# Layer-0 preparation of an adaLN and mixture-of-experts kernel in two halves

## The chip, the cores and the metric

The kernel runs on one core of a Trainium2 chip. The metric is the device time of one execution in microseconds. TensorE (PE), VectorE (DVE), ScalarE (ACT) and GpSimd (POOL) each run one instruction stream in order; SyncE (SP) issues most DMAs, also in order. The streams meet only at semaphores.

## The reference, cut to what matters

Two layers are computed, each a per-sequence product of x with a gathered matrix and then a feed-forward network of experts, with residual sums. The change touches layer 0 alone. With N = 2048 tokens, D = 512, hidden width 2048, E = 8 experts of rank 8, for both choices k of the router:

```python
def _L0_ffn_ref(hidden_states, W_r, b_r, W1, b1, W2, b2, A1, B1, A2, B2):
    probs = jax.nn.softmax(x @ W_r.T + b_r, axis=-1)
    w_topk, idx_topk = jax.lax.top_k(probs, K)
    base1 = x @ W1.T + b1
    u1 = jnp.einsum('nd,erd->ner', x, A1)
    for k in range(K):
        oh = jax.nn.one_hot(idx_topk[:, k], E, dtype=x.dtype)
        z1 = (u1 * oh[:, :, None]).reshape(N, E * R)
        h = act(base1 + z1 @ B1_rf * SCALING)
        u2 = jnp.einsum('nf,erf->ner', h, A2)
        z2 = (u2 * oh[:, :, None]).reshape(N, E * R)
        y = h @ W2.T + b2 + z2 @ B2_rf * SCALING
        res = res + w_topk[:, k:k + 1] * y
```

Layer 1 is a per-sequence product with a bias, and a routed expert network beside a shared one. It is the same before and after.

## The kernel before

The 2048 tokens are four super-tiles (s, or n in the preparation) of 512, each of TPS = 4 tiles of 128; J = 16 is the number of tiles. The 2048 hidden units are FT = 16 chunks f of 128, so layer 0 has 64 hidden tiles i = 16 s + f. Every fp32 operand is kept as a high and a low half, and a product is three matmuls: high by high, high by low, low by high.

**Preparation.** For each super-tile `cond_x(n)` gives the transposed product in ps_y (TensorE); ScalarE's `high_x` and VectorE's `low_x` split it. `router_and_u1(n)` (12 matmuls) gives the router's logits and the low-rank product u1 in ps_h; ScalarE copies the logits to lg_t, `logit_rows` (TensorE) turns them, `logits` (VectorE) brings them to SBUF. u1 is copied by VectorE (`u1_rows`) and a second time by ScalarE. `route(k, js)` on VectorE is a chain of small operations with one `Exp` on ScalarE between them: it finds both experts and both weights. The first call does the 4 tiles of super-tile 0, the second the 12 others. It ends with the masks' operands (mexp_first, mexp_rest) which `masks` on TensorE turns and ScalarE copies to m_base and m_step; `place_z` on VectorE multiplies u1 by them. `rho_rows` turns the ratio of the weights; SP stores it to DRAM and `load_weights` brings it back over all partitions as wb.

**Weights.** Of each chunk SP loads w_raw; ScalarE (`high_w2`, `high_w1`), VectorE (`low_w2`) and GpSimd (`low_w1`) split it into w2_hi, w2_lo (kept) and w_hl (two buffers), and SP stores w_hl to w1s_d, from where super-tiles 1 to 3 load it again. `high_w1(f)` for f of 2 or more waits for the store that frees its buffer.

**Hidden tiles.** `step` on TensorE is: `hidden` of tile i (12 matmuls on x, 2 on z), half of `down` of tile i - 1 (8), `second` (2), the other half of `down` (8): 32 matmuls. ScalarE does two gelus for each tile, VectorE `hidden_tile` (multiply by wb, add, and two splits). PSUM is full: ps_h has 2 banks, ps_y 4 (which `down` accumulates in over a super-tile), ps_u 2. In `super_tile(0)` all of `rho_rows(1)` and `masks(1)` to `masks(3)` stand between `second` of tile 1 and `down` of tile 0, and use ps_y.

The order on each engine is written out by hand. TensorE's before is: cond_x 0 and 1, router 0, cond_x 2, router 1, cond_x 3, router 2, rho_rows 0, masks 0, router 3, logit_rows 2, hidden_x 0, logit_rows 3, hidden_x 1, hidden_z, super-tiles.

Of the kernel before, what the change touches and what calls it, by code (L numbers as in the profile page):

```python
# [23 lines left out]
def adaln_ffn(nc, x, itok0, itok1, side, cond0, router0, router0_b, w1b, b1, b2, b2s,  # L24
# [34 lines left out]
    with ExitStack() as top:  # L59
# [47 lines left out]
        rho_t = [sb(f"rho_t{k}", [n, P]) for k, n in enumerate((TPS, J - TPS))]  # L107
# [30 lines left out]
        zz = sb("zz", [P, SUP])  # L138
        zq = sb("zq", [P, SUP])
# [95 lines left out]
        bd_in_act = sem("bd_in_act")  # L235
# [5 lines left out]
        u1_twice = sem("u1_twice")  # L241
# [150 lines left out]

        def lgt_at(n, j=0):

            return (n * TPS + j) * 2 * E
# [32 lines left out]
        def _(sp):  # L428
# [8 lines left out]
            def load_bd(n):  # L437
                for j in range(TPS):
                    load_block(sp, n, j, 0, bd_in[n][0])
# [26 lines left out]
            load_bd(1)  # L466
            load_w1(0)
            for n in range(2, NS):
                sp.wait_ge(cond_done, 1 + (n - 1) * DC)
                load_x(n)  # L470
                load_bd(n)
            load_w1(1)
            for n in range(2, NS):
                sp.wait_ge(xt_lo_done, 4 + (n + 1) * DC)
                for half, dst in zip(xt_of(n), (xt_hi_d, xt_lo_d)):
                    sp.dma_start(dst[n - 2], half.rearrange("p c n -> p (c n)").bitcast(F32)).then_inc(xt_st[n % 2], 16)
                if n == 2:
                    sp.wait_ge(wt_sb, 1)
                    sp.dma_start(wrow_d[0:TPS, :], rho_t[0][:]).then_inc(wrow_st, 16)
                    sp.wait_ge(wrow_st, 16)  # L480
                    load_weights(0)
# [25 lines left out]

            for s in range(NS):
                for f in range(FT):
                    nxt = s * FT + f + 2  # L510
                    if nxt < FT:
                        load_w1(nxt)
                    if s == 0:
                        store_w1(f)
                    if FT <= nxt <= STEPS:
                        load_w1s(nxt)
                    if s == 0 and f == 2:
                        sp.wait_ge(wt_sb, 2)
                        sp.dma_start(wrow_d[TPS:J, :], rho_t[1][:]).then_inc(wrow_st, 16)
                        sp.wait_ge(wrow_st, 32)  # L520
                        load_weights(1)
                    if s and f == 1:
                        store_x1(s - 1)
                    if s == 0 and f == XRES_AT:

                        sp.wait_ge(g_done, 3)
# [71 lines left out]
        def _(pool):  # L598
# [160 lines left out]
        def _(act):  # L759
# [5 lines left out]
            for j in range(TPS // 2, TPS):  # L765
                load_block(act, 0, j, 1, bd_in_act)
# [34 lines left out]
            def exps(k, js):  # L801
# [3 lines left out]
            def masks(n):  # L805
                s, k = n // 2, n % 2
                act.wait_ge(mt_done, n + 1)
                nc.scalar.copy((m_base, m_step)[k][:, s * SUP:(s + 1) * SUP], ps_y[:, n % 4, :]).then_inc(mt_read, 1)

            def rho_rows(k):  # L810
                act.wait_ge(w01t_done, k + 1)
                nc.scalar.copy(rho_t[k][:], ps_u[0:(TPS, J - TPS)[k], 1, (k + 2) * P:(k + 3) * P]).then_inc(wt_sb, 1)
# [20 lines left out]
            def gelus(i, f, u, sums=None):  # L833
                b = bias1[:, f:f + 1]
                act.wait_ge(a_done, i + 1)
                act.wait_ge(g_done, i + 1)
                nc.scalar.activation(h0[u][:], ps_h[:, u, :], ACT.Gelu_apprx_tanh, bias=b).then_inc(h0_done, 1)  # L837
                if sums is not None:
                    move_sums(sums)
                act.wait_ge(z_done, i + 3)  # L840
                act.wait_ge(g1_done, i + 1)
                nc.scalar.activation(h1[u][:], ps_h[:, u, :], ACT.Gelu_apprx_tanh, bias=b).then_inc(h1_done, 1)  # L842

            for f in range(FT):
                gelus(f, f, f % 2)
                if f == 1:
                    rho_rows(1)
                    for n in range(2, 2 * NS):
                        masks(n)
# [3 lines left out]
            def move_sums(s):  # L853

                for j, t in enumerate((zz, zq)):
# [120 lines left out]
        def _(dve):  # L976
# [7 lines left out]
            dve.wait_ge(small_in, 16 * 5)  # L984
            nc.vector.tensor_copy(ur_hi[:, :, 0:ER + E], ur_raw[:]).then_inc(split_small, 1)
            nc.vector.tensor_copy(b2s_hi[:], b2s_raw[:]).then_inc(split_small, 1)
            dve.wait_ge(split_small, 2)
            nc.vector.tensor_tensor(ur_hi[:, :, ER + E:UR], ur_raw[:, :, ER:ER + E],
                                    ur_hi[:, :, ER:ER + E].bitcast(F32), ALU.subtract).then_inc(split_small, 1)
            nc.vector.tensor_tensor(u1_lo[:], ur_raw[:, :, 0:ER], ur_hi[:, :, 0:ER].bitcast(F32), ALU.subtract)\  # L990
                .then_inc(split_small, 1)
            nc.vector.tensor_tensor(b2s_lo[:], b2s_raw[:], b2s_hi[:].bitcast(F32), ALU.subtract).then_inc(split_small, 1)

            def low_x(n):
                hi, lo = xt_of(n)
                for c in range(DC):
# [26 lines left out]
            def softmax(rt, rc, parts, bias, r_max, r_exp, js=slice(0, J), turn=1):  # L1023
# [6 lines left out]
                tt(l, p, over_e(m), ALU.subtract).then_inc(r_max, 1)  # L1030
                dve.wait_ge(r_exp, turn)
# [847 lines left out]
```

## Time and profile before

| what | value |
|---|---|
| median of 3 runs | 1081.24 us (1078.67 to 1088.08) |
| the profiled execution, its own time | 1079.91 us |
| its span, first to last instruction | 1078.3 us |
| mean granted TensorE clock | 0.986 |
| TensorE busy | 1025.1 us |
| VectorE busy | 545.7 us |
| ScalarE busy | 308.9 us |
| GpSimd busy | 353.6 us |

The execution's own time is 1.6 us longer than its span. Engines overlap, so busy times don't add up. A start in a row is counted from the span's first instruction.

### The profile page before, as it was taken

The numbers are of one execution on the slowest core, as the hardware profiler recorded it, in microseconds if no ns is written. First come the engines' busy times: TensorE is split into PE (matmuls) and PEld (weight loads), VectorE is DVE, ScalarE is ACT, GpSimd is POOL, SyncE is SP. The second block draws the span as 40 slices with busy tenths as digits, with TensorE's granted clock in tenths as the row PEclk, the third lists the DMA queues.
The fourth block names the chain that finished last, engine by engine and source line by source line (L and its number), as shares of the span: only waits on it lengthen the run. The fifth ranks groups of instructions, "written<-read, shape, count | busy, mean of one in ns | idle before, by whom it ended". The sixth has DMA issues, their size and how long they took to land.

```text
span 1078.3 us, 14931 instructions
## 1 busy us (share of the span) xinstructions
PE 1025.1 (95%) x4922; PEld 842.2 (78%) x4923; DVE 545.7 (51%) x888; ACT 308.9 (29%) x542; POOL 353.6 (33%) x349
## 2 busy tenths in 40 slices
PE   7879999999999999999978999999999999999993
PEld 5668888788878888788845777778878989998993
DVE  3777776555475445654475443484553344452100
ACT  2443332211121121212123110210034444454551
POOL 3113335430000000000024000003058889888873
PEclk9989999999999999999999999999999999999997
DMA  7566652543434334432336110101446665556433
GB/s 210 205 184 215 193 183 87 164 142 128 146 117 139 125 140 154 156 128 88 107 130 235 42 40 1 40 1 55 162 159 158 153 148 115 148 130 158 76 61 39
DMA packets 51371, 136.42 MB, mean 127 GB/s; under 512 B 8788, under 2 KB 10052, under 8 KB 50820
## 3 DMA queue, kind: packets, MB, share of 16 engines
q1 hardware_dynamic: 37700, 109.55, 30.1%
q0 software_dynamic: 12368, 25.68, 12.0%
q10 hardware_dynamic: 1264, 0.72, 0.4%
q8 instruction: 19, 0.31, 0.1%
q14 instruction: 20, 0.16, 0.0%
HBM read 96.85 MB, written 39.07 MB: 126 GB/s over the span
## 4 chain that ended last, share of the span: by engine, by line
PE 72%; DMA 8%; DVE 6%; POOL 6%; issue 3%; SPq 1%; ACT 1%; PEldq 0%; POOLq 0%; DVEq 0%; PEld 0%; ACTq 0%
DMA out_x<-yt,slot_tok 7%; PE ps_y L1543 6%; PE ps_y L1545 6%; PE ps_y L1544 6%; PE ps_h L1507 5%; PE ps_h L1506 5%; PE ps_h L1505 5%; PE ps_u L1551 3%; PE ps_u L1550 3%; PE ps_y L1694 2%; PE ps_y L1695 2%; PE ps_h L1678 2%; POOL xg L700 2%; PE ps_h L1679 2%; PE ps_h L1680 2%
## 5 line engine op out<-in xcount | busy, mean ns | idle before, releaser
L1103 DVE TENSOR_TENSOR h<-h,wb 128x512 f32<-128x512 f32 x64 | 45.6, 713 | 176.0 <-ACT h L842 175.9
L837 ACT ACTIVATE h<-ps_h,bias 128x512 f32<-128x512 f32 x64 | 44.1, 690 | 238.8 <-PE ps_h L1514 238.7
L1543 PE MATMUL ps_y<-w_hi,g_hi 128*128 (+1 forms) x256 | 102.3, 400 | 3.0 <-DVE g_lo L1111 3.0
L1505 PE MATMUL ps_h<-xt_hi,w_hl 128*128 128x512 f32 x256 | 100.6, 393 | 2.0 <-POOL w_hl L625 2.0
L1545 PE MATMUL ps_y<-w_hi,g_lo 128*128 (+1 forms) x256 | 101.6, 397 | 0.0
L1544 PE MATMUL ps_y<-w_lo,g_hi 128*128 (+1 forms) x256 | 101.5, 396 | 0.0
L1507 PE MATMUL ps_h<-xt_hi,w_hl 128*128 128x512 f32 x256 | 101.0, 394 | 0.0
L1506 PE MATMUL ps_h<-xt_lo,w_hl 128*128 128x512 f32 x256 | 100.9, 394 | 0.0
L1329 DVE CAST eg_hi<-e_raw 128x704 fp32r<-128x704 f32 x32 | 21.1, 717 | 123.5 <-PE ps_y L1790 112.4
L842 ACT ACTIVATE h<-ps_h,bias 128x512 f32<-128x512 f32 x64 | 44.0, 688 | 116.3 <-PE ps_h L1527 116.3
L711 POOL DMA_INDIRECT out_x<-yt,slot_tok x39 | 63.4, 1625 | 27.7 <-DMA out_x<-yt,slot_tok 18.5
L643 POOL DMA_DIRECT2D s_raw<-in_sgu x8 | 4.3, 547 | 195.1 <-DVE g_lo L1111 190.6
L717 POOL TENSOR_TENSOR xg_lo<-xg_f,xg_hi 128x512 fp32r<-128x512 f32 x39 | 59.5, 1526 | 14.9 <-ACT xg_f L924 13.4
L1543 PEld LDWEIGHTS ps_y<-w_hi,g_hi 128*128 128x128 f32 x256 | 48.3, 188 | 15.5 <-DVE g_lo L1111 2.7
L1505 PEld LDWEIGHTS ps_h<-xt_hi,w_hl 128*128 128x128 f32 x256 | 48.5, 190 | 13.3 <-ACT lg_t L797 2.1
L1116 DVE TENSOR_TENSOR g_lo<-h,g_hi 128x512 fp32r<-128x512 f32 x64 | 56.9, 888 | 2.2
L1545 PEld LDWEIGHTS ps_y<-w_hi,g_lo 128*128 128x128 f32 x256 | 48.3, 189 | 11.7
L1544 PEld LDWEIGHTS ps_y<-w_lo,g_hi 128*128 128x128 f32 x256 | 48.4, 189 | 11.4
L1506 PEld LDWEIGHTS ps_h<-xt_lo,w_hl 128*128 128x128 f32 x256 | 48.3, 189 | 11.2
L1507 PEld LDWEIGHTS ps_h<-xt_hi,w_hl 128*128 128x128 f32 x256 | 48.5, 189 | 10.5
L729 POOL TENSOR_TENSOR rgt_lo<-rgt_f,rgt_hi 128x384 fp32r<-128x384 f32 x39 | 54.8, 1406 | 5.3 <-ACT rgt_f L942 5.3
L1760 PE MATMUL ps_y<-eg_hi,xg_hi 128*128 x156 | 53.5, 345 | 0.0
(303 smaller groups left out, 2485.1 us busy)
## 6 DMA issues: line engine op xcount, KB each, us to landing
w_hl<-w1s_d SPq DMA_DIRECT2D x49, 704.0 KB, 4.1
w1s_d<-w_hl SPq DMA_DIRECT2D x16, 704.0 KB, 6.0
e_raw<-in_wgu SPq DMA_DIRECT2D x8, 1408.0 KB, 7.6
w_raw<-in_w1b SPq DMA_DIRECT2D x16, 608.0 KB, 4.7
x_in<-in_x SPq DMA_DIRECT2D x4, 1024.0 KB, 7.1
xres<-in_x SPq DMA_DIRECT2D x16, 256.0 KB, 4.4
x_d<-xres SPq DMA_DIRECT2D x4, 1024.0 KB, 7.5
acc<-x_d SPq DMA_DIRECT2D x4, 1024.0 KB, 7.8
```

Of the source, the lines that this page charges most:

```text
L711: pool.indirect_dma_start(out=out, in_=yt[t % 4][:], in_offset=None, out_offset=bass.IndirectOffsetOnAxis(ap=slot_tok[:, t:t + 1], axis=0) ...
L717: nc.gpsimd.tensor_tensor(xg_lo[:].rearrange("p c n -> p (c n)"), xg_f[:], xg_hi[:].rearrange("p c n -> p (c n)").bitcast(F32), ALU.subtract)\
L729: nc.gpsimd.tensor_tensor(rgt_lo[:].rearrange("p c n -> p (c n)"), rgt_f[:], rgt_hi[:].rearrange("p c n -> p (c n)").bitcast(F32), ALU.sub ...
L1103: tt(h1[u][:], h1[u][:], wb[:, v, :], ALU.mult).then_inc(gch, 1)
L1116: tt(g1_lo[u][:], h1[u][:], g1_hi[u][:].bitcast(F32), ALU.subtract).then_inc(g1_done, 1)
L1505: mm(ps_h[:, u, :], w_chunk(u, 0, c), xt_hi[v][:, c, :], start=(c == 0), stop=False)
L1506: mm(ps_h[:, u, :], w_chunk(u, 0, c), xt_lo[v][:, c, :], start=False, stop=False)
L1507: mm(ps_h[:, u, :], w_chunk(u, 1, c), xt_hi[v][:, c, :], start=False, stop=False)
L1543: mm(ps_y[:, j, :], g_hi[u][:, cols], sl(w2_hi), start=first, **kw)
L1544: mm(ps_y[:, j, :], g_hi[u][:, cols], sl(w2_lo), start=False, **kw)
L1545: mm(ps_y[:, j, :], g_lo[u][:, cols], sl(w2_hi), start=False, **kw)
L1760: mm(o, xg_hi[:, c, :], w(eg_hi, c), start=(c == 0), stop=False)
```

## The change

1. Routing goes by halves of 8 tiles (super-tiles 0 and 1, then 2 and 3). The first route is woven with the splits of super-tiles 2 and 3 (`meanwhile`, `split`); the second stands on VectorE behind hidden tile 1, and its `Exp` on ScalarE behind the first four gelus.
2. Masks are made by super-tile: 0 and 1 in the preparation (ps_y), 2 and 3 in super-tiles 1 and 2 (ps_u), each with its own operands (`spread_masks`).
3. On TensorE routers 0 and 1 stand together; hidden_x of tile 1 goes ahead of rho_rows and masks 0; router 3, into ps_u, has both `second` between its halves; then masks 1, logit_rows 3 and `down` of tile 0.
4. ScalarE copies u1 twice straight from PSUM, and splits w1 and w2 of chunks 0 and 1 ahead of the masks; VectorE's `low_w2` 0 and 1 also go ahead.
5. On SP both stores of split x go ahead of the store of rho and of wb; chunks 2 and 3 of the weights and the second wb follow. Some loads of bd change queue.

```diff
             def logits_and_u1(n):
                 act.wait_ge(u1_done, n + 1)
                 act.wait_ge(lgt_done, n)
-                nc.scalar.copy(lg_t[:], ps_h[ER:UR, n % 2, :]).then_inc(lgt_cp, 1)
-                act.wait_ge(u1_read, n + 1)
-                nc.scalar.copy(u1t[ER:P, n * SUP:(n + 1) * SUP], u1t[0:ER, n * SUP:(n + 1) * SUP]).then_inc(u1_twice, 1)
+                rows = u1_bank(n)
+                nc.scalar.copy(lg_t[:], rows[ER:UR]).then_inc(lgt_cp, 1)
+                nc.scalar.copy(u1t[0:ER, n * SUP:(n + 1) * SUP], rows[0:ER])
+                nc.scalar.copy(u1t[ER:P, n * SUP:(n + 1) * SUP], rows[0:ER]).then_inc(u1_read, 1)
...
             high_x(0)
             high_x(1)
             logits_and_u1(0)
+            high_w1(0)
+            logits_and_u1(1)
             high_x(2)
-            exps(0, slice(0, TPS))
-            logits_and_u1(1)
+            exps(0)
             high_x(3)
+            high_w1(1)
+            high_w2(0)
+            high_w2(1)
             logits_and_u1(2)
+            nc.scalar.activation(h0[0][:], zero16[:], ACT.Gelu_apprx_tanh).then_inc(warm, 1)
             rho_rows(0)
             masks(0)
-            masks(1)
-            for f in range(2):
-                high_w2(f)
-                high_w1(f)
-            logits_and_u1(3)
-            exps(1, slice(TPS, J))
-            nc.scalar.activation(h0[0][:], zero16[:], ACT.Gelu_apprx_tanh).then_inc(warm, 1)
             act.wait_ge(warm, 1)
...
+            for f in range(2):
+                gelu_first(f, f, f)
+            for f in range(2):
+                gelu_second(f, f, f)
+            high_w1(2)
+            logits_and_u1(3)
+            masks(1)
+            high_w2(2)
+            high_w2(3)
+            high_w1(3)
+            exps(1)
+            for f in range(2, FT):
                 gelus(f, f, f % 2)
...
+                    if s == 1 and f == 1:
+                        rho_rows(1)
                     gelus(s * FT + f, f, f % 2, s - 1 if f == 1 else None)
+                    if s + 1 < NS and f == 1:
+                        masks(s + 1)
...
             low_x(0)
+            split_constants()
             low_x(1)
-            u1_rows(0)
-            low_x(2)
             logits(0)
-            route(0, slice(0, TPS))
-            u1_rows(1)
+            low_x(2, range(0, 2))
             logits(1)
-            low_x(3)
-            u1_rows(2)
+            route(0, split=True)
+            spread_masks(0, [m[:, 0:TPS] for m in mexp_first])
+            low_w2(0)
+            low_w2(1)
             logits(2)
             place_z(0)
             place_z(1)
-            u1_rows(3)
-            low_w2(0)
-            low_w2(1)
-            logits(3)
-            route(1, slice(TPS, J))
+            spread_masks(1, [m[:, TPS:2 * TPS] for m in mexp_first])
...
                         hidden_tile(f, v, f % 2)
+                        if f == 0:
+                            logits(3)
...
+                        if f == 1:
+                            route(1)
...
+            sp.wait_ge(wt_sb, 1)
+            sp.dma_start(wrow_d[0:J // 2, :], rho_t[0][:]).then_inc(wrow_st, 16)
+            sp.wait_ge(wrow_st, 16)
+            load_weights(0)
+            for f in range(2):
+                load_w1(f + 2)
+                store_w1(f)
+            load_weights(1)
...
             cond_x(0)
             cond_x(1)
             router_and_u1(0)
-            cond_x(2, between=0)
             router_and_u1(1)
-            cond_x(3, between=1)
+            logit_rows(0)
+            cond_x(2, between=1)
+            cond_x(3)
             router_and_u1(2)
+            pe.wait_ge(lgt_cp, 2)
+            pe.wait_ge(u1_read, 2)
+            hidden_x(1, 0, 1, None)
+            pe.wait_ge(xt_lo_done, 4 + NS * DC)
             rho_rows(0)
-            pe.wait_ge(xt_lo_done, 4 + NS * DC)
             masks(0)
-            router_and_u1(3)
             logit_rows(2)
-            for u in range(2):
-                pe.wait_ge(lgt_cp, 3 + u)
-                pe.wait_ge(u1_read, 3 + u)
-                if u:
-                    logit_rows(3)
-                hidden_x(u, 0, u, None)
+            pe.wait_ge(u1_read, 3)
+            hidden_x(0, 0, 0, None)
             hidden_z(0, 0)
+            hidden_z(0, 1)
+
+            def seconds():
+                second(0, 0, 0)
+                second(1, 0, 1)
+
+            router_and_u1(3, between=seconds)
             for s in range(NS):
                 super_tile(s, s % 2)
```

In `super_tile(s)` for s of 1 or more TensorE now does `second` of the first tile, `sums_end(s - 1)`, for s = 1 `rho_rows(1)`, `second` of the second tile, `masks(s + 1)`, and then `down`.

## Rows read from the trace of the kernel before

**Rows 1.** Page, part 1: busy time, share and instructions.

```profile
PE 1025.1 (95%) x4922; PEld 842.2 (78%) x4923; DVE 545.7 (51%) x888; ACT 308.9 (29%) x542; POOL 353.6 (33%) x349
```

**Rows 2.** Windows of 30 us: stretch, each engine's busy us, then clock, DMA share, GB/s.

```profile
30.00:60.00 30.00, 22.83 (x118) 16.35 (x116) 22.70 (x65) 13.22 (x24) 4.23 (x4) 0.94 0.62 226
60.00:90.00 30.00, 26.06 (x118) 20.87 (x119) 21.05 (x35) 12.33 (x22) 8.74 (x8) 0.89 0.57 174
90.00:120.00 30.00, 30.00 (x132) 24.37 (x131) 24.24 (x32) 10.67 (x16) 10.24 (x9) 1.00 0.68 211
```

**Rows 3.** Timeline of TensorE: start, duration, instruction, idle before and releaser.

```profile
39.24 0.27 PE L1480 MATMUL ps_u<-ident,rho 128*4 128x128 f32 x1
41.85 0.62 PE L1490 MATMUL ps_y<-ident,mexp_first 128*128 128x128 bf16 x8 [2.33 <-DVE w_lo L998]
...
47.61 0.55 PE L1505 MATMUL ps_h<-xt_hi,w_hl 128*128 128x512 f32 x1 [2.00 <-POOL w_hl L625]
...
58.71 0.50 PE L1526 MATMUL ps_h<-z_step,w_hl 128*128 128x512 f32 x1 [1.41 <-ACT h L837]
...
61.99 0.80 PE L1526 MATMUL ps_h<-z_step,w_hl 128*128 128x512 f32 x1 [2.55 <-ACT h L837]
...
63.34 2.25 PE L1490 MATMUL ps_y<-ident,mexp_rest 128*128 128x128 bf16 x24
67.53 0.47 PE L1543 MATMUL ps_y<-w_hi,g_hi 128*128 128x512 f32 x1 [1.95 <-DVE g_lo L1111]
...
72.87 0.39 PE L1505 MATMUL ps_h<-xt_hi,w_hl 128*128 128x512 f32 x1
...
80.28 0.39 PE L1505 MATMUL ps_h<-xt_hi,w_hl 128*128 128x512 f32 x1
```

**Rows 4.** Windows of 1 us (columns as in rows 2).

```profile
49.00:50.00 1.00, 1.00 (x4) 0.81 (x3) 1.00 (x1) 0.00 (x0) 0.78 (x1) 0.50 1.01 426
...
70.00:71.00 1.00, 1.00 (x4) 0.81 (x3) 0.86 (x3) 0.00 (x0) 0.00 (x0) 0.50 0.98 180
```

**Rows 5.** Timeline of VectorE.

```profile
39.31 2.48 DVE L998 TENSOR_TENSOR w_lo<-ps_y,w_lo 128x512 fp32r<-128x512 f32 x4 [1.17 <-ACT w_lo L792]
...
46.10 1.81 DVE L1071 TENSOR_TENSOR zf<-u1t,m_base 128x512 f32<-128x512 f32 x1 [0.22 <-DVE lg L1007]
...
50.36 0.69 DVE L1071 TENSOR_TENSOR zf<-u1t,m_step 128x512 f32<-128x512 f32 x1
...
54.55 0.26 DVE L1026 TENSOR_TENSOR rt_p<-lg 128x96 f32<-128x96 f32 x1
...
62.20 1.08 DVE L1061 TENSOR_SCALAR mexp_rest<-rt_l 128x1536 bf16<-128x1536 f32 x1
```

**Rows 6.** Timeline of ScalarE.

```profile
8.52 1.28 ACT L792 ACT_TABLE_LOAD   x1 [8.52 <-issue]
14.47 0.58 ACT L792 CAST xt_hi<-ps_y 128x512 fp32r<-128x512 f32 x1 [4.68 <-PE ps_y L1456]
...
56.01 1.28 ACT L830 ACT_TABLE_LOAD   x1
...
60.57 0.78 ACT L787 CAST w_hl<-w_raw 128x704 fp32r<-128x704 f32 x1
```

**Rows 7.** Waits of SP's queue, 0 to 140 us: total us, times, longest.

```profile
SPq L448 <- DMA wrow_d<-rho_t: 5.7, 2, 4.8
```

**Rows 8.** DMA issues, 43 to 62 us: times, size, median us to landing.

```profile
w1s_d<-w_hl SPq DMA_DIRECT2D x2, 704.0 KB, 7.0
...
xt_lo_d<-w_lo SPq DMA_DIRECT2D x1, 1024.0 KB, 7.7
```

**Rows 9.** Timeline where super-tile 1 begins.

```profile
187.75 0.68 ACT L837 ACTIVATE h<-ps_h,bias 128x512 f32<-128x512 f32 x1
...
189.77 0.40 PE L1526 MATMUL ps_h<-z_step,w_hl 128*128 128x512 f32 x1
...
190.75 0.19 PEld L1543 LDWEIGHTS ps_y<-w_hi,g_hi 128*128 128x128 f32 x1 [0.80 <-DVE g_lo L1111]
```

More of the change, by code:

```diff
@@ L138, in adaln_ffn @@
         zz = sb("zz", [P, SUP])
+        spread = ExitStack()
+        sb_spread = tensors(spread)
+        mexp_next = [sb_spread(f"mexp_next{k}", [P, TPS, P], BF16) for k in range(2)]
+        spread.close()
         zq = sb("zq", [P, SUP])
@@ L437, in load_bd @@
             def load_bd(n):
-                for j in range(TPS):
+                for j in range(TPS // 2 if n == 2 else TPS):
                     load_block(sp, n, j, 0, bd_in[n][0])
@@ L466, in _ @@
             load_bd(1)
+            load_bd(2)
+            sp.wait_ge(cond_done, 1 + DC)
+            load_x(2)
             load_w1(0)
[L468 to L471, printed above, removed]
+            load_bd(3)
+            sp.wait_ge(cond_done, 1 + 2 * DC)
+            load_x(3)
             load_w1(1)
@@ L845, in _ @@
                 gelus(f, f, f % 2)
[L846 to L849, printed above, removed]
                 if f + 2 < FT:
@@ L1477, in rho_rows @@
                 pe.wait_ge(w01_ok, k + 1)
-                pe.wait_ge(wt_sb, k)
-                first, many = ((0, TPS), (TPS, J - TPS))[k]
-                nc.tensor.transpose(ps_u[0:many, 1, (k + 2) * P:(k + 3) * P], rho[:, first:first + many], ident[:])\
-                    .then_inc(w01t_done, 1)
+                nc.tensor.transpose(rho_bank(k), rho[:, half_of(k)], ident[:]).then_inc(w01t_done, 1)
             def masks(s):
-                pe.wait_ge(mexp_ok, 2 if s == 0 else 4)
-                for n in (2 * s, 2 * s + 1):
-                    if n >= 4:
-                        pe.wait_ge(mt_read, n - 3)
-                    spread = mexp_rest[n % 2][:, (s - 1) * TPS:s * TPS] if s else mexp_first[n % 2][:]
+                if s == 1:
+                    pe.wait_ge(wt_sb, 1)
+                if s == 2:
+                    pe.wait_ge(wt_sb, 2)
+                for k in range(2):
+                    pe.wait_ge(mexp_ok, 2 * s + k + 1)
+                    expanded = mexp_first[k][:, s * TPS:(s + 1) * TPS] if s < 2 else mexp_next[k][:]
                     for j in range(TPS):
-                        last = mm(ps_y[:, n % 4, j * P:(j + 1) * P], spread[:, j], ident16[:], start=True, stop=True)
+                        last = mm(mask_bank(s, k)[:, j * P:(j + 1) * P], expanded[:, j], ident16[:],
+                                  start=True, stop=True)
                     last.then_inc(mt_done, 1)
@@ L1549, in down @@
                 hi, lo = ((g_hi, g_lo), (g1_hi, g1_lo))[half]
+                if first and s == 0:
+                    pe.wait_ge(lu_done, NS)
+                    pe.wait_ge(u1_read, NS)
+                if first and s in (1, 2):
+                    pe.wait_ge(mt_read, 2 * s + 3 + half)
                 mm(ps_u[:, half, :], a2, hi[u][:], start=first, **kw)
@@ L1576, in super_tile @@
                     hidden_x(base + 1, v, 1, rows)
-                hidden_z(s, 1)
-                second(base, s, 0)
-                if s:
+                    hidden_z(s, 1)
+                    second(base, s, 0)
                     sums_end(s - 1)
-                second(base + 1, s, 1)
-                if s == 0:
-                    rho_rows(1)
-                    for k in range(1, NS):
-                        masks(k)
-                    pe.wait_ge(wt_sb, 2)
-                    pe.wait_ge(mt_read, 2 * NS)
+                    if s == 1:
+                        rho_rows(1)
+                    second(base + 1, s, 1)
+                if s + 1 < NS:
+                    masks(s + 1)
+                if s == 0:
+                    logit_rows(NS - 1)
                 down(base, 0, 0, 0, s)
```

160 lines of the change are left out of this document (92 added, 68 removed).

## The prediction

> **What bounds the kernel now.** I read the page's busy times first: TensorE is busy for 1025.1 of 1078.3 us [rows 1], so only about 53 us could be won without taking matmuls away, and this change takes none away that count. Then the windows of 30 us, to see where those 53 us lie that the change can reach. From 90 us TensorE is busy in all of its 30 us at full clock; from 30 to 90 it is idle for 11.1 us (7.17 and 3.94) and its clock is 0.94 and 0.89 [rows 2]. So the change acts on a stretch that ends at about 80 us. The timeline of TensorE shows what is waited for there: 2.33 us for the split of super-tile 3, 2.00 for GpSimd's split of w1, 1.41 and 2.55 for ScalarE's first gelus, 1.95 for VectorE's first g_lo [rows 3], 10.2 us together. Behind such gaps the granted clock falls to 0.50, the 1.2 GHz level [rows 4]; in the two stretches in which it does, matmuls of 512 columns start 0.43 us apart and not 0.23. At 0.50 TensorE has lost half of what it does: some 1.7 us for each stretch of 3.4 us.
>
> I use two marks. The mark **step 2** is the start of hidden tile 2 at 72.87 us, the mark **step 3** that of tile 3 at 80.28 [rows 3]. The step between them has 32 matmuls in 7.41 us, 0.23 each, and later steps are the same. What is won at step 3 is won in the end, save what is handed to the later super-tiles.
>
> **The new order, worked through.** *Up to router 2.* TensorE's work is the same, and before it ended with the transpose of rho at 39.24 [rows 3]. Router 1 now fills the 0.5 us in which cond_x 2 waited for its DMA. I take 38.8 us: no gain worth naming. ScalarE's extra copies (u1 from PSUM) and its early `high_w1(0)` fit in gaps.
>
> *Hidden_x of tile 1.* It needs both w1 splits. ScalarE's second is behind `high_x(3)`, 36.6 to 37.4, GpSimd's then takes 1.9 to 2.5 us: 39.9. Twelve matmuls of 0.23: 42.7. The gap is 1.1 us instead of 2.33 plus 2.00.
>
> *Routing, first half.* VectorE's chain for 8 tiles, with the four splits of super-tile 3 (2.48 us, [rows 5]) inside it, is the next thing late. It has 22 small operations up to the ratio of the weights. Before, 54.55 to 62.20 were 24 of them and one spread of some 0.9 us for 12 tiles, so 0.28 us each [rows 5]; with 8 tiles I take 0.255. From 32.2 us the sum is 22 × 0.255 + 4 × 0.62 (super-tile 3) + 2 × 0.62 (the rest of super-tile 2) = 9.3 us, to 41.5, and GpSimd's split of w1 runs at that time: one operation took 1.81 us with GpSimd busy where the same takes 0.69 [rows 5], so one hit, 1.1 us (bounds: none, or two): rho and the last split at about 42.6. The masks' operands follow at 43.6, `low_w2` of 0 and 1 at 44.9. TensorE turns rho and mask 0 to 44.4, then logit_rows 2, hidden_x 0 (2.8 us, to 47.6), four z products (0.9), half of router 3 (1.4), both `second` (0.9), the other half (1.4), mask 1 (0.6): 52.8 us. `place_z` twice is 3.8 us from 45.3 (GpSimd idle), in time. What stood as two waits for gelu, 1.41 and 2.55, is now behind router 3: gone.
>
> *What is late next: the store that frees w_hl.* ScalarE has `high_w1(2)` ahead of the copy of router 3's logits. It waits for the store of chunk 0, and that stands on SP behind both stores of x, the store of rho, and wb. I follow this queue. x of super-tile 3 is split at 42.6, so its two stores of 1 MB are issued at about 42.8; rho is in SBUF at 43.4 and its store goes right behind them. Before, the two waits for a rho store were 0.9 and, behind other transfers, 4.8 us (5.7 in all, [rows 7]); with 2 MB ahead I take 4.0: 47.5. Then wb, the load of chunk 2, and the store of chunk 0 at 48.5. Such a store took 7.0 us at the median [rows 8]; the first of these was issued at 54.13, and ScalarE took the buffer without a wait at 60.57 [rows 6], so at most 6.4. I take 6.7: 55.2. Queued behind that wait on ScalarE are the logits and u1 of super-tile 3, mask 1 and the splits of w2 2 and 3; who waits for them is TensorE, for logit_rows 3, from 52.8. So: `high_w1(2)` to 56.0, logits copied 56.6, rows turned 57.1, a new gap of over 4 us. `down` of tile 0 is 16 × 0.23 = 3.7: step 2 at 60.9, against 72.87. Before, its masks for 12 tiles (2.25 us, [rows 3]) stood here too; 8 of 24 remain, ahead of the gap.
>
> *Routing, second half.* VectorE takes logits 3, waits for w2's split (60.0), does tile 1 (g_lo 62.8, all of it 64.0), another w2 split (64.6), then four operations of route: 65.7. ScalarE's `Exp` ends at 66.0. Gelu's table is loaded again: a load is 1.28 us [rows 6]. The load of Exp's table costs nothing, as ScalarE waits there anyway and a load runs ahead of the wait of its instruction: the first one ran at 8.52, the copy behind it waited for TensorE until 14.47 [rows 6]. Gelu of tile 2 then ends at 68.0, and `second` of tile 2, which TensorE reaches at 60.9 + 3.2 + 1.8 = 65.9 at full clock, starts at 68.2: a second gap of 2.3 us. With 2 + 8 more matmuls step 3 starts at 70.5. To that I add 1.5 for the clock: two gaps could cost 1.7 each behind them, but what is lost ahead of a wait costs nothing. Bounds 0 and 3.4. **Step 3 at 72.0**, 8.3 us earlier than before.
>
> On tables the traces show 1.28 us and the next instruction right behind. The Trainium skill (ScalarE: Activation LUTs, What ACT_TABLE_LOAD costs) counts 2.66 us for a switch, the drain with it, and advises to batch calls by table set, which this change stops doing: it would make the sum 1.4 us worse. In this trace the gap behind the load at 56.01 is too small for that drain, so the row decides.
>
> *Handed to later super-tiles.* Masks 2 and 3 are 16 small matmuls, 16 × 2.25 / 24 = 1.5 us, on TensorE where it has little to wait. At super-tile 1 gelu of tile 17 ran at 187.75, during `sums_end`, and `second` went at 189.77 [rows 9]; now ScalarE first waits for rho_rows(1), behind `sums_end`, copies it and only then starts that gelu: `second` is 1.4 us late. Of this and the mask, up to 0.80 at each of two places falls in the wait for g_lo that stood there [rows 9]. VectorE's two spreads (0.8 us) fall in its own idle time. Sum 1.5 + 1.4 - 1.0 = **1.9 us** (bounds 1.0 and 3.3).
>
> **Sum.** 8.3 - 1.9 = 6.4 us. Against the profiled execution's own time of 1079.91 (1.6 us over its span) that is **1073.5 us**. The median shown is 1.3 above that execution; a measurement of this kernel can tell about 1%, 11 us, from nothing.
>
> **Rivals.** (a) *The rho store is quick and the clock holds.* It speaks for this that one such store took 0.9 us, against it that 2 MB stand ahead now. Then 3.1 us off the queue, 0.3 off the store and 1.5 off the clock come on top: 1073.5 - 4.9 = 1068.6. Chance 0.18.
>
> (b) *Routing's second half gives back more.* For it: the chain now stands between tiles 1 and 2, so VectorE comes to tile 2 at about 71 us, when GpSimd splits w1 of chunk 4, and an operation then takes 1.1 us more [rows 5]; two such hits and one more slow stretch (1.7) give 3.9 us: 1077.4. Against it: a step leaves VectorE about 1.5 us. Chance 0.22. A switch of the length that the Trainium skill gives on the page named above falls among these times.
>
> (c) *The end on the other side: the SP queue.* If what was moved together on SP runs at the mean of 60 to 90 us, 174 GB/s [rows 2], and not at 426 [rows 4], then 2.1 MB of x end at 42.8 + 12.1 = 54.9, and wb, chunk 2 and the store (1.6 MB, 9.2 us) at 64.1. All after it is 8.9 us later: 1082.4. It decides from 61.6 us on: if chunk 0's store lands later than that, the change loses. Against it: in 1 us windows with a full queue the DMAs move over 400 GB/s. Chance 0.10.
>
> (d) *It doesn't do what it says*: if mask 1 and router 3 find an earlier wait (a bank of ps_y or ps_u not yet free), they stand in the open, 2.8 + 0.6 us: 1076.9. It lies in (b)'s times; both banks are free by my walk some us before. Chance 0.05.
>
> **How the numbers follow.** The forecast itself, 1071 to 1077, has 0.45. The range 1068.5 to 1081 takes in (a), (b), (d) and the bounds of rho's store (0.9 to 4.8) and of the clock, and leaves out most of (c). Faster by over 1% is below 1070.4: most of (a) and a little of the forecast's early side, 0.19. Slower by over 1% needs more than (c): 0.04. Within 1%: 0.77.
>
> **What the changed profile would show.** TensorE: hidden_x of tile 1 at about 40 us with a gap of near 1; no gap between the z products and `second`; a gap of 4 us ahead of logit_rows 3, ended by ScalarE's copy; step 2 at 61, a gap ahead of `second` of tile 2 that ends with gelu, step 3 at 72. ScalarE: two more table loads, the first hidden; `high_w1(2)` idle before it for the store of w_hl. At super-tile 1 a gap of over 1 us ahead of `second`. The prediction is wrong if `high_w1(2)` doesn't wait (a), if step 3's lead has gone by tile 5 (b), or if that store lands after 61.6 (c).

## The result and the profile after

The changed kernel takes 1074.63 us (median of 10 runs, 1070.94 to 1081.08) against 1080.74 us (10 runs) of the kernel before: a ratio of 0.9947, 95% interval 0.9921 to 0.9973. The forecast was 1073.5 us. The profiled execution has a span of 1071.6 us. One execution each of e9_w2_back (5790.24 us) and e10_spread (2060.74 us) took far longer than all others, for no reason that the record shows, and neither is counted below. TensorE's busy time, from the page, answers to [rows 1]:

```profile
PE 1020.5 (95%) x4922; PEld 840.5 (78%) x4923; DVE 534.3 (50%) x888; ACT 314.1 (29%) x548; POOL 352.1 (33%) x349
```

The matmuls are the same 4922. TensorE is busy for 4.6 us less; in a second trace of the changed kernel (e11_after_again) it is 1022.3 us, 2.8 less, so part of this is scatter. The windows of 30 us answer to the first two of [rows 2]:

```profile
30.00:60.00 30.00, 21.39 (x130) 16.71 (x131) 20.70 (x53) 15.87 (x28) 3.47 (x4) 0.90 0.63 245
60.00:90.00 30.00, 28.71 (x114) 22.55 (x113) 22.86 (x48) 13.15 (x21) 7.06 (x7) 0.93 0.57 167
```

From 30 to 90 us TensorE is now idle for 9.9 us (8.61 and 1.29) instead of 11.1, and more of the work is in the first window. By the clock column TensorE's clock is at 0.50 for as long as before, 10.2 us, but differently placed: before, in three stretches (at about 48, 62 and 68 us) in which TensorE was at work for all but 0.5 us; now in one stretch from 54.3 to 64.5, in which it has nothing to do until 59. Work at the low clock fell by about 4 us, and as it runs there at half speed, that is some 2 us of time (an estimate from these windows). TensorE's timeline shows one large gap where five middling ones stood [rows 3]:

```profile
38.98 0.47 PE L1563 MATMUL ps_h<-xt_hi,w_hl 128*128 128x512 f32 x1 [0.71 <-ACT lg_t L827]
...
50.44 0.62 PE L1547 MATMUL ps_y<-ident,mexp_first 128*128 128x128 bf16 x8
58.96 0.60 PE L1484 MATMUL ps_u<-ident,lg_t 16*128 16x16 f32 x4 [7.90 <-ACT lg_t L827]
59.49 0.80 PE L1605 MATMUL ps_y<-w_hi,g_hi 128*128 128x512 f32 x1
...
65.58 0.39 PE L1563 MATMUL ps_h<-xt_hi,w_hl 128*128 128x512 f32 x1
...
71.05 0.50 PE L1584 MATMUL ps_h<-z_step,w_hl 128*128 128x512 f32 x1 [0.27 <-ACT h L865]
...
73.48 0.39 PE L1563 MATMUL ps_h<-xt_hi,w_hl 128*128 128x512 f32 x1
...
77.88 0.50 PE L1605 MATMUL ps_y<-w_hi,g_hi 128*128 x1 [1.03 <-DVE g_lo L1161]
...
82.17 0.39 PE L1563 MATMUL ps_h<-xt_hi,w_hl 128*128 128x512 f32 x1
```

A step is the start of a hidden tile on TensorE. Step 2 (65.58) comes 7.3 us earlier than before, step 3 (73.48) 6.8 us, step 4 (82.17 against 87.67) 5.5 us. TensorE's gap of 7.90 names ScalarE's copy of the logits; what ScalarE waited for is in its own timeline (compare [rows 6]):

```profile
57.52 0.78 ACT L816 CAST w_hl<-w_raw 128x704 fp32r<-128x704 f32 x1 [7.48 <-DMA w1s_d<-w_hl]
58.33 0.58 ACT L827 COPY lg_t<-ps_u 16x512 f32<-16x512 f32 x1
...
66.72 1.28 ACT L834 ACT_TABLE_LOAD   x1
68.74 0.26 ACT L834 ACTIVATE rt_q<-rt_l 128x64 f32<-128x64 f32 x1 [0.74 <-DVE rt_l L1077]
69.02 1.28 ACT L865 ACT_TABLE_LOAD   x1
70.31 0.69 ACT L865 ACTIVATE h<-ps_h,bias 128x512 f32<-128x512 f32 x1
```

`high_w1(2)` stood 7.48 us for the store that frees its buffer, with the logits queued behind it, as forecast. SP's queue shows why the store was late:

```profile
40.92 0.32 SPq L499 DMA_DIRECT2D xt_hi_d<-w_lo  x1
41.28 0.43 SPq L499 DMA_DIRECT2D xt_lo_d<-w_lo  x1
42.41 0.33 SPq L527 DMA_DIRECT2D wrow_d<-rho_t  x1
49.29 0.34 SPq L469 DMA_DIRECT2D wb<-wrow_d  x1
...
50.15 0.43 SPq L503 DMA_DIRECT2D w1s_d<-w_hl  x1
```

Between the issue of rho's 4 KB (42.41) and that of wb (49.29), which waits for them, lie 6.9 us: the 2 MB of x stand ahead. Whether they are the cause is tested in e2 below. Where super-tile 1 begins ([rows 9]), `second` of tile 17 waits for a gelu:

```profile
184.26 0.27 PE L1536 MATMUL ps_u<-ident,rho 128*8 128x128 f32 x1
185.46 0.50 PE L1584 MATMUL ps_h<-z_step,w_hl 128*128 128x512 f32 x1 [0.93 <-ACT h L865]
...
186.46 0.48 PE L1605 MATMUL ps_y<-w_hi,g_hi 128*128 128x512 f32 x1
```

**A common zero.** The first loads land up to 3 us apart from trace to trace: the first matmul of router 0 starts at 21.46 here, 21.80 before, and between 21.6 and 24.7 in the experiments. So times in the experiments are counted from that matmul. The last mark is the first matmul of the last `sums_end`, at layer 0's end. Two traces of the same kernel (changed and e11; e6 and e12) differ at these marks by up to 0.6 us, so less than that is not read as an effect. From the last mark to the end of the span it is 522.6 to 530.0 us in these traces, though layer 1 is the same in all; so the marks settle effects in layer 0 that the whole time can't. The ratio is to the kernel before in the same series, and each series had a chip of its own (e1 to e4; e5 to e8; e9 to e12).

| from router 0, us | down of tile 0 | step 4 | last sums | ratio to before, 95% |
|---|---|---|---|---|
| before | 45.7 | 65.9 | 528.7 | |
| changed | 38.0 | 60.7 | 524.7 | 0.9947 (0.9921 to 0.9973) |
| e11_after_again | 38.3 | 61.3 | 525.2 | 0.9955 (0.9936 to 0.9975) |
| e1_act_late | 36.2 | 60.2 | 524.2 | 0.9913 (0.9883 to 0.9943) |
| e2_rho_first | 33.1 | 56.4 | 520.4 | 0.9926 (0.9896 to 0.9956) |
| e3_router_back | 38.5 | 61.2 | 525.1 | 0.9953 (0.9925 to 0.9981) |
| e4_rho_turn | 38.6 | 61.6 | 524.8 | 0.9926 (0.9898 to 0.9955) |
| e5_queue_clear | 32.3 | 55.7 | 518.9 | 0.9910 (0.9880 to 0.9941) |
| e6_all | 32.3 | 52.5 | 516.5 | 0.9885 (0.9849 to 0.9922) |
| e7_no_exp | 38.3 | 61.7 | 525.7 | 0.9962 (0.9936 to 0.9987) |
| e8_all_router_back | 33.6 | 55.0 | 519.0 | 0.9904 (0.9871 to 0.9936) |
| e9_w2_back | 38.4 | 61.2 | 525.1 | 0.9975 (0.9955 to 0.9994) |
| e10_spread | 38.2 | 59.3 | 524.1 | 0.9957 (0.9940 to 0.9975) |
| e12_all_again | 32.5 | 52.7 | 516.7 | 0.9872 (0.9853 to 0.9892) |

### The profile page after: what moved, and what is told of

The parts are those of the page before. It is cut to its first block, busy times and chain, and to the rows that moved or that the text cites. A ratio compares the mean times of both kernels' runs of the same rounds, so it can differ in the third digit from the quotient of the medians.

```text
span 1071.6 us, 14937 instructions
## 1 busy us (share of the span) xinstructions
PE 1020.5 (95%) x4922; PEld 840.5 (78%) x4923; DVE 534.3 (50%) x888; ACT 314.1 (29%) x548; POOL 352.1 (33%) x349
## 4 chain that ended last, share of the span: by engine, by line
PE 80%; DMA 5%; DVE 5%; POOL 4%; issue 2%; ACT 1%; SPq 1%; PEldq 0%; POOLq 0%; DVEq 0%; PEld 0%; ACTq 0%
PE ps_y L1605 5%; PE ps_y L1607 5%; PE ps_y L1606 5%; PE ps_h L1565 5%; PE ps_h L1564 5%; PE ps_h L1563 5%; DMA out_x<-yt,slot_tok 3%; PE ps_u L1618 3%; PE ps_u L1617 3%; PE ps_y L1766 2%; PE ps_h L1837 2%; PE ps_y L1767 2%; PE ps_y L1837 2%; PE ps_y L1832 2%; PE ps_y L1833 2%
## 5 line engine op out<-in xcount | busy, mean ns | idle before, releaser
L1564 PEld LDWEIGHTS ps_h<-xt_lo,w_hl 128*128 128x128 f32 x256 | 48.1, 188 | 11.1
L1832 PE MATMUL ps_h<-eg_hi,xg_hi 128*128 x156 | 50.9, 327 | 2.7 <-ACT xg_hi L968 1.8
```

Of the source, the lines that this page charges most:

```text
L1564: mm(ps_h[:, u, :], w_chunk(u, 0, c), xt_lo[v][:, c, :], start=False, stop=False)
L1832: mm(o, xg_hi[:, c, :], w(eg_hi, c), start=(c == 0), stop=False)
```

## Experiments on the gap: ScalarE's order and SP's queue

**e1_act_late.** ScalarE's order alone:

```diff
-            high_w1(2)
             logits_and_u1(3)
             masks(1)
+            high_w1(2)
```

> On ScalarE the split of w1 of chunk 2 goes behind the logits and masks of super-tile 3's router. Theory (ScalarE waits 7.5 us for the store of w_hl and holds the logits back): logit_rows 3 then starts at about 51.5 us and not at 59.0, and the next thing late is wb (VectorE's tile 0 starts at 54.2, g_lo at 57.0), so down of tile 0 starts at 57.1 instead of 59.5; step 3 at about 71.5 instead of 73.5, time 2 us less (ratio to before 0.993). Rival (GpSimd's split of chunk 2 and routing's second half are the bound behind it, not the logits): step 2 moves, step 3 stays at 73.5, ratio 0.995.

In TensorE's timeline the gap has moved from the logits to `down` of tile 0:

```profile
51.47 0.41 PE L1484 MATMUL ps_u<-ident,lg_t 16*128 16x16 f32 x4 [0.21 <-ACT lg_t L827]
57.85 0.79 PE L1605 MATMUL ps_y<-w_hi,g_hi 128*128 128x512 f32 x1 [5.97 <-DVE g_lo L1161]
70.55 0.50 PE L1584 MATMUL ps_h<-z_step,w_hl 128*128 128x512 f32 x1 [2.15 <-ACT h L865]
```

The logits are turned at 51.47, as the theory says, and wb is next: VectorE's tile 0 started at 55.05, after 6.5 us of waiting for it. `down` is 1.9 us earlier, but ahead of `second` of tile 2 there is now a gap of 2.15 us, and step 4 is only 0.5 us earlier, within the scatter: the rival is right about the end, and for the reason it gives. Its ratio, 0.9913, is lower than its trace accounts for.

**e2_rho_first.** SP's order alone:

```diff
+            store_xt(2)
...
             sp.wait_ge(wt_sb, 1)
             sp.dma_start(wrow_d[0:J // 2, :], rho_t[0][:]).then_inc(wrow_st, 16)
             sp.wait_ge(wrow_st, 16)
             load_weights(0)
             for f in range(2):
                 load_w1(f + 2)
                 store_w1(f)
+            store_xt(3)
             load_weights(1)
```

> On SP the two stores of x of super-tile 3 go behind the store of rho, wb, and the loads and stores of w1 that follow. Theory (the rho store took 6.9 us because 2 MB stood ahead of it): the rho store lands in about 1.3 us, wb is there at 48, the store that frees w_hl lands at about 51, ScalarE's wait falls from 7.5 to about 1, down of tile 0 starts at 53 to 54, step 2 at 57.5, step 3 at 68 to 69: 4.5 to 5.5 us less than the changed kernel, ratio to before 0.990. Rival (routing's second half gives it back): step 3 at 72 or later, ratio 0.994.

SP's queue (router 0 is at 24.66 here), and TensorE's gap:

```profile
45.56 0.33 SPq L529 DMA_DIRECT2D wrow_d<-rho_t  x1
47.84 0.34 SPq L469 DMA_DIRECT2D wb<-wrow_d  x1
...
48.70 0.43 SPq L505 DMA_DIRECT2D w1s_d<-w_hl  x1
```

```profile
57.39 0.41 PE L1487 MATMUL ps_u<-ident,lg_t 16*128 16x16 f32 x4 [3.14 <-ACT lg_t L830]
```

(`store_xt(n)` is the loop's body for super-tile n.) The rho store now holds the queue for 2.3 us instead of 6.9, the gap falls from 7.90 to 3.14, and step 4 and the last sums are 4.3 us earlier from router 0: the first theory stands, a little below its 4.5 to 5.5 us. The median ratio shows only 2 to 3 of these us; where the rest goes is open. The theory's landing time for the store of w_hl was too short: issued at 48.70, it freed ScalarE at 55.96. At tile 2 gaps of 1.64 and 1.04 us are left.

**e5_queue_clear.** Both orders, the stores of w_hl 0 and 1 ahead of rho, and the edit of e4 below:

```diff
+            store_xt(2)
+            for f in range(2):
+                store_w1_early(f)
             sp.wait_ge(wt_sb, 1)
...
             load_weights(0)
             for f in range(2):
                 load_w1(f + 2)
-                store_w1(f)
+            store_xt(3)
             load_weights(1)
```

> SP stores w_hl of chunks 0 and 1 ahead of everything that follows x of super-tile 2, then rho and wb, then the loads of chunks 2 and 3, and x of super-tile 3 last; ScalarE has the split of chunk 2 behind the masks, and the turned rho behind the gelu of tile 17. Times are counted from router 0's first matmul (the changed kernel: down of tile 0 at 38.0, step 4 at 60.7, last sums at 524.7; the second experiment 33.1, 56.4, 520.4). Theory (queue and ScalarE's wait are the whole gap): down of tile 0 at 31.5, set by g_lo; step 4 at 52, since routing's second half still stands between tiles 1 and 2; last sums at 515; ratio to before 0.986. Rival (wb, spread over 128 partitions, moves slowly and is the bound wherever it stands): down of tile 0 at 33 or later, ratio 0.990.

```profile
54.40 0.42 PE L1493 MATMUL ps_u<-ident,lg_t 16*128 16x16 f32 x4 [0.21 <-ACT lg_t L836]
56.85 0.50 PE L1614 MATMUL ps_y<-w_hi,g_hi 128*128 128x512 f32 x1 [2.04 <-DVE g_lo L1170]
```

The gap is down to 0.21 and 2.04 us. `down` of tile 0 at 32.3 lies between the two forecasts, and what is left of the wait is the rival's: VectorE stood 2.58 us for wb (whether wb is slow because it is a broadcast is another matter, taken up in the last section). The theory missed its later marks: step 4 is at 55.7 and not 52, the last sums at 518.9 and not 515. `down` of tile 0 took 5.4 us instead of 3.7, with the clock at 0.50 in part, and the gaps at tile 2 are 1.72 and 1.01 us.

## Experiments on routing's second half

**e6_all.** As e5, and the route in pieces:

```diff
-                        if f == 1:
-                            route(1)
+                        route_piece(f)
...
-            exps(1)
             for f in range(2, FT):
                 gelus(f, f, f % 2)
...
+                if f == 3:
+                    exps(1)
```

The pieces are the four operations up to `Exp` (f = 2), the three that normalize (3), the first choice (4), the second (6), and the ratio with the masks' operands (7). SP loads the residual from f = 9 and not from f = 3, as it shares the memory.

> As e5_queue_clear, and routing's second half in five pieces behind tiles 2, 3, 4, 6 and 7, its Exp behind tile 3's gelus; the loads of the residual go behind it. Theory (a step of tiles leaves VectorE some 1.5 us, and the chain of 6 us in one piece does not fit): no gap ahead of second of tile 2 nor ahead of down of tile 2, step 4 at 50.0 from router 0, last sums at 513, ratio to before 0.984, 2 us less than e5_queue_clear. Rival (the pieces push g_lo over its slack in five steps): five small gaps of 0.5 us, and no gain over e5_queue_clear.

```profile
56.95 0.50 PE L1638 MATMUL ps_y<-w_hi,g_hi 128*128 128x512 f32 x1 [2.12 <-DVE g_lo L1195]
```

This is the last gap of TensorE that its timeline lists up to 100 us. Both gaps at tile 2 are gone, step 4 is 3.2 us earlier than in e5 and the last sums 2.4 us. Instead of the rival's five small gaps there is one, of 0.54 us at 103.2. Both of the theory's marks were missed, 50.0 by 2.5 us and 513 by 3.5, as e5 missed its own by 3.7 and 3.9; against e5 it gains 3.2 and 2.4 us where 2 were forecast.

**e10_spread.** The same pieces alone in the changed kernel, with the `Exp` and the loads of the residual moved as in e6.

```diff
-                        if f == 1:
-                            route(1)
+                        route_piece(f)
...
-            exps(1)
...
+                if f == 3:
+                    exps(1)
```

> The changed kernel with routing's second half in five pieces behind tiles 2, 3, 4, 6 and 7 and its Exp behind tile 3's gelus, nothing else changed. Theory: down of tile 0 stays at 38.0 from router 0, the gaps of 0.27 and 1.03 ahead of second and down of tile 2 go, step 4 at 59.2 instead of 60.7, last sums at 523.3. Rival (the tiles catch up later anyway, so the gaps only move): last sums at 524.5.

Step 4 at 59.3 is as forecast and both gaps at tile 2 are gone. At the last sums, 524.1 against 524.7 and 525.2 of the two traces of the changed kernel, 0.6 to 1.1 us are left, little more than the scatter, of 1.4 forecast: part is given back, as the rival says, and one gap of 0.54 us ahead of a later `down` has appeared.

**e7_no_exp.** Is it the table switch that costs there?

```diff
-                nc.scalar.activation(rt["q"][:, js], rt["l"][:, js], ACT.Exp).then_inc(r_exp, 1)
+                nc.scalar.activation(rt["q"][:, js], rt["l"][:, js], ACT.Copy if k else ACT.Exp).then_inc(r_exp, 1)
```

> The changed kernel with a plain copy in place of the second Exp, so that gelu's table stays: the weights of super-tiles 2 and 3 are then wrong. Theory (the first load runs while ScalarE waits, the second ends 0.3 us after TensorE gets there): the gap ahead of second of tile 2 goes, the one ahead of down of tile 2 stays as VectorE's chain sets it, step 4 at 60.3 to 60.7 from router 0, ratio as for the changed kernel. Rival (a switch costs 2.7 us with its drain): step 4 1.5 us or more earlier.

The gap ahead of `second` went, as the theory says. But step 4 was not earlier: it is 1.0 us *later* than in the first trace of the changed kernel and 0.4 later than in the second, since the gap ahead of `down` of tile 2 grew to 2.68 us. VectorE's timeline, and below it GpSimd's:

```profile
67.54 1.50 DVE L1075 TENSOR_TENSOR rt_p<-rt_p,rb_rows 128x64 f32<-128x64 f32 x1
69.08 0.22 DVE L1076 TENSOR_REDUCE rc_m<-rt_p 128x8 f32<-128x64 f32 x1
...
74.51 1.59 DVE L1117 TENSOR_TENSOR oh_step<-rt_oh,oh_base 128x64 f32<-128x64 f32 x1
```

```profile
67.39 1.57 POOL L653 TENSOR_TENSOR w_hl<-w_raw,w_hl 128x640 fp32r<-128x640 f32 x1
...
74.45 1.57 POOL L653 TENSOR_TENSOR w_hl<-w_raw,w_hl 128x640 fp32r<-128x640 f32 x1
```

Two operations that take 0.23 us elsewhere took 1.50 and 1.59, each beside a split of w1 on GpSimd. The changed kernel has two such hits as well:

```profile
67.47 1.23 DVE L1077 TENSOR_TENSOR rt_l<-rt_p,rc_m 128x64 f32<-128x64 f32 x1
...
75.80 1.93 DVE L1161 TENSOR_TENSOR g_lo<-h,g_hi 128x512 fp32r<-128x512 f32 x1
```

These two stand beside GpSimd's splits of 67.06 and 75.38 and take 1.23 us instead of 0.22 and 1.93 instead of 0.69. Without the tables TensorE was earlier (step 3 by 0.7 and 1.3 us against the two traces), and with it GpSimd's second split, which then fell on the end of the chain and not on g_lo behind it. VectorE's path to g_lo of tile 2 became no shorter, so the time won at `second` was lost again at `down`. Each of the two switches is a load of 1.28 us, and the first was hidden. Together they were worth the gap ahead of `second`, 0.27 us in the first trace and 0.92 in the second, and nothing at step 4. There is no room in ScalarE's timeline for the 2.66 us that the Trainium skill (ScalarE: Activation LUTs, What ACT_TABLE_LOAD costs) counts: a load at 69.02 ends at 70.30 and gelu starts at 70.31.

## Experiments on two of the change's moves

**e3_router_back.** The placing of router 3 around `second` undone in the changed kernel:

```diff
             logit_rows(2)
+            pe.wait_ge(lu_done, 3)
+            router_and_u1(3)
             pe.wait_ge(u1_read, 3)
             hidden_x(0, 0, 0, None)
             hidden_z(0, 0)
             hidden_z(0, 1)
-            router_and_u1(3, between=seconds)
+            second(0, 0, 0)
+            second(1, 0, 1)
```

> Only the placing of the fourth router product is undone: all 12 of its matmuls stand ahead of hidden_x of tile 0, nothing between the first matmuls of the tiles and second. Theory (TensorE has a gap of 7.9 us behind it that the weights' store ends, so where the product stands is worth nothing): step 3 within 0.5 us of 73.5, ratio to before 0.9947 as for the changed kernel. Rival (the placing is what won the time: 2.8 us of matmuls cover the gelus): 2 to 3 us more, ratio 0.997.

```profile
52.77 0.50 PE L1584 MATMUL ps_h<-z_step,w_hl 128*128 128x512 f32 x1 [0.38 <-ACT h L865]
61.46 0.60 PE L1484 MATMUL ps_u<-ident,lg_t 16*128 16x16 f32 x4 [6.91 <-ACT lg_t L827]
```

The gap ahead of the logits is 1.0 us shorter and 1.0 us of new gaps stand ahead of it (the 0.38 shown, and 0.65 ahead of router 3). Last sums 525.1, ratio 0.9953: the placing earns nothing here.

**e8_all_router_back.** The same edit in e6_all.

> As e6_all with the fourth router product whole and ahead of hidden_x of tile 0. Theory (once the queue is clear, its 2.8 us of matmuls do cover the first gelus): down of tile 0 and step 4 are 2.5 to 3 us later than in e6_all, ratio to before 0.003 higher. Rival (the same time either way, as VectorE's way to g_lo and the turned logits bound it): less than 0.7 us later.

Step 4 is 2.5 us later than in e6_all and the last sums 2.4 us, as the theory says; the ratio is 0.0019 higher, inside its interval. `down` of tile 0 is only 1.2 us later; the other 1.2 us are lost in `down` itself, which takes 6.6 us instead of 5.4, with the clock at 0.50 through nearly all of it. So in these traces the placing has its worth once nothing longer hides it.

**e9_w2_back.** VectorE's early splits of w2 undone:

```diff
-            low_w2(0)
-            low_w2(1)
             logits(2)
             place_z(0)
             place_z(1)
+            low_w2(0)
+            low_w2(1)
```

> The changed kernel with VectorE's splits of w2 0 and 1 back behind place_z of super-tile 0. Theory (they let SP load chunks 2 and 3, but SP is behind the rho store until 28 us after router 0 anyway): z is ready 1.2 us earlier where nothing waits for it, wb and the weights are loaded when they were, down of tile 0 within 0.3 us of 38.0 from router 0, last sums within 0.5 of 524.7. Rival (splitting them ahead is what starts the loads early): the load of chunk 2 and all behind it 1 us or more later.

Down of tile 0 at 38.4, last sums at 525.1: the same as the changed kernel again on the same chip (38.3 and 525.2). Its median, 1076.29 us, is 3.2 us above that kernel's 1073.08, with intervals that overlap; nothing in layer 0's trace answers to it, and I leave it open.

**e4_rho_turn.** At super-tile 1, on ScalarE:

```diff
-                    if s == 1 and f == 1:
-                        rho_rows(1)
...
                 gelu_first(i, f, u)
                 if sums is not None:
+                    if sums == 0:
+                        rho_rows(1)
                     move_sums(sums)
```

> At super-tile 1 ScalarE does the first gelu of tile 17 ahead of the copy of the turned rho instead of behind it. Theory: the gap of 0.93 us ahead of second of tile 17 goes and up to 0.4 us come back as wait for g_lo: 1.0 us less in the distance from second of tile 16 to down of tile 16 (5.0 now, 4.2 before). In the whole time too small for a verdict. Rival (g_lo of tile 16 was the bound there anyway): that distance stays at 5.0.

```profile
187.16 0.27 PE L1536 MATMUL ps_u<-ident,rho 128*8 128x128 f32 x1
187.19 0.48 PE L1584 MATMUL ps_h<-z_step,w_hl 128*128 128x512 f32 x1
...
188.45 0.47 PE L1605 MATMUL ps_y<-w_hi,g_hi 128*128 128x512 f32 x1
```

The gap of 0.93 is gone. From the sums' first matmul to `down` of tile 16 it is now 4.1 us, against 5.0 in the changed kernel and 3.8 before (the 4.2 in the expectation counts from `second` of tile 16, the 5.0 from the sums).

## The best version beside the changed kernel

**e11_after_again.**

> The changed kernel again, beside the kernel with all edits on the same chip. Both theories: ratio to before 0.9947 within its interval, last sums 524.7 from router 0.

**e12_all_again.**

> The kernel with all edits of e6_all again. Theory (the 8.2 us that its last sums are earlier from router 0 are real and the rest of the kernel is the same): its median is 6 to 9 us below that of the changed kernel on the same chip, ratio to before 0.987. Rival (layer 1 gives part of it back, as its tail was 4.5 us longer in one trace): less than 4 us below.

On one chip, with 27 runs of the kernel before (1079.21 us): the changed kernel 1073.08 us (12 runs), the kernel with all edits 1064.43 us (5 runs, 1063.28 to 1067.98), ratio to before 0.9872 (0.9853 to 0.9892). That is 8.7 us below the changed kernel, and its last sums are 8.5 us earlier: it beats both kernels. From the last sums to the end it takes 528.0 us against 527.8, so in this pair of traces the rest of the kernel gives nothing back.

## Why the prediction was right, step by step

The mechanism held, and so did the sum: 6.4 us were forecast, 6.1 measured, and the span is 6.7 us shorter. The terms were less exact than the sum.

- *Up to mask 1* I gave 52.8 us; TensorE was done at 51.06. The gap ahead of hidden_x of tile 1 was 0.71 instead of 1.1. Of GpSimd's hits on VectorE one took place, for 0.5 us (an operation of 0.77 instead of 0.22) and not 1.1.
- *The store that frees w_hl* was named as the next thing late, and it was. Its size was off: the rho store held SP for 6.9 us, 6.5 of them a wait, where I took 4.0 and gave 4.8 as bound. The 4.8 was a wait with 1.3 MB ahead of it; 2 MB were ahead here. The store then took 7.4 us to release ScalarE instead of 6.7. So the gap was 7.9 us and not "over 4". e2 shows the cause: with these 2 MB moved behind it the same store took 2.3 us.
- *The clock*: I added 1.5 us behind the two gaps together. `down` of tile 0 took 6.1 us (59.49 to 65.58) instead of 3.7, as the large gap brought the clock down to 0.50. The cost of 2.4 us is above what I took and inside the bounds of 0 and 3.4. I also counted only two low stretches in the kernel before; its windows have a third, from 61.5 to 64.9 us, with the clock at 0.50.
- *Routing's second half*: ScalarE's `Exp` started at 68.74 and gelu of tile 2 ended at 71.0, 3 us later than forecast, since what they wait for was late by about that much; the gap ahead of `second` was 0.27 and not 2.3, because TensorE was late too. Step 3 came at 73.48, 1.5 us behind the forecast. Then TensorE stood 1.03 us ahead of `down` of tile 2, and step 4 came 8.7 us after step 3 instead of 7.4. So 1.3 us of rival (b), priced at 3.9, were true. Both of its hits took place, for 1.0 and 1.2 us (the lines under e7), but its slow stretch of the clock did not, and the rest of the hits fell where TensorE wasn't waiting.
- *Handed to later super-tiles*: from step 4 to the last sums 5.2 us of lead fell to 4.0, a cost of 1.1 us instead of 1.9: at super-tile 1 it is 1.2, mask included, and at super-tile 2 nothing, where the mask falls into the wait that stood there.
- The remaining 0.3 and 2.3 us of the shorter span lie ahead of router 0 and behind the last sums, where layer 1 is the same in both. Two traces of one kernel differ there by up to 2.9 and 2.3 us, so both are inside the scatter. Layer 0's gain was 4.0 us in one trace and 3.5 in the other, less than the 6.4 forecast, and that the whole came out at 6.1 is in part luck. The medians of two series (10 and 12 runs) both show 6.1 us; the 2 us between this and layer 0's gain stay unexplained.

Rival (a) is refuted: the store was slower than in any row. Rival (c) did not come to its point: the store landed at 57.5, before 61.6, but it was nearer to it than I thought. Rival (d), that the moved router 3 and mask 1 find an earlier wait and stand in the open, was wrong: TensorE has no gap ahead of either. But the placing of router 3 was worth nothing all the same, for another reason, the longer wait behind it: undone one at a time, neither it nor the early splits of w2 move layer 0 (e3, e9). That the gaps of before are gone because the long route for 12 tiles and its masks no longer stand ahead of `down` of tile 0 is read from the two traces; no run undid that part alone, so it is argued and not shown.

## What to carry to other kernels

A move that covers a wait is worth nothing while a longer wait ends behind it; find what each engine's in-order stream has queued ahead of the result that the bound engine needs (here a buffer's split ahead of the logits, and 2 MB of stores ahead of 4 KB). Issue the small transfer that someone waits for, and the stores that free buffers, ahead of the bulk that nobody needs yet. A serial chain of small operations that is due only much later goes in pieces into the slack of the steady loop.

## What the runs showed of the hardware

- *The first loads after an idle queue moved slowly, a broadcast to 128 partitions or not.* Windows of 1 us of the changed kernel, the first wb issued at 49.29 and the second, behind the weights, at 52.09 (the last three columns are the clock, the DMA share and GB/s):

```profile
50.00:51.00 1.00, 1.00 (x11) 0.56 (x9) 0.00 (x0) 0.04 (x1) 0.00 (x0) 1.00 0.37 119
51.00:52.00 1.00, 0.06 (x2) 0.00 (x0) 0.00 (x0) 0.00 (x0) 0.00 (x0) 1.00 0.68 81
52.00:53.00 1.00, 0.00 (x0) 0.00 (x0) 0.00 (x0) 0.00 (x0) 0.00 (x0) 1.00 0.67 94
53.00:54.00 1.00, 0.00 (x0) 0.00 (x0) 0.00 (x0) 0.00 (x0) 0.00 (x0) 1.00 0.77 300
54.00:55.00 1.00, 0.00 (x0) 0.00 (x0) 0.69 (x1) 0.00 (x0) 0.00 (x0) 0.62 1.04 430
...
60.00:61.00 1.00, 1.00 (x4) 0.72 (x3) 0.00 (x0) 0.97 (x3) 0.20 (x1) 0.50 0.35 133
...
63.00:64.00 1.00, 1.00 (x4) 0.73 (x3) 0.79 (x3) 0.00 (x0) 0.00 (x0) 0.50 0.58 102
64.00:65.00 1.00, 1.00 (x5) 0.81 (x4) 0.96 (x2) 0.00 (x0) 0.00 (x0) 0.76 1.01 272
```

  For 3 us the queue moved 81 to 119 GB/s with 2.6 MB of loads and stores of w1 issued right behind wb, and 430 as soon as wb was through (VectorE starts on it at 54.23). That looks like the price of the broadcast, but the second wb, of the same form, moved at the ordinary rate: its rows are all that the window from 60 to 61 holds, 133 GB/s at a DMA share of 0.35, where the first had 81 at 0.68. And the kernel before has the same slow start with plain loads of w1, issued at 53.75 with no wb near:

```profile
54.00:55.00 1.00, 1.00 (x6) 0.82 (x5) 0.83 (x4) 0.00 (x0) 0.00 (x0) 1.00 0.60 83
55.00:56.00 1.00, 1.00 (x6) 0.81 (x5) 0.61 (x3) 0.28 (x1) 0.00 (x0) 1.00 0.82 141
```

  No run separates the idle queue from the broadcast. For a forecast: a price per byte from the middle of a full queue is too low for the first load after a pause.
- *The clock.* It fell to 0.50, the 1.2 GHz level, while TensorE was idle (0.62 from 54 to 55 us, in the same rows) and was still there when work came back at 59; it rose between 64 and 65, some 5 us into the work. The long gap cost 7.9 us and another 2.4 us behind it.
- *VectorE and GpSimd.* An operation on 64 elements in each partition took 1.23 to 1.59 us beside a GpSimd split that reads SBUF (e7 and both traces of the changed kernel), and 0.22 to 0.23 without; one on 512 elements took 1.93 instead of 0.69.
